# The low halves of the gelu's output: VectorE and GpSimd by turns, or VectorE alone from PSUM

## What is computed

```python
for l in range(attn_w.shape[0]):
    scores = leaky(si[:, :, None] + sj[:, None, :] + attn_b[l])       # masked, softmax
    agg = jnp.einsum('bij,bjd->bid', attn, x)
    h = layernorm(x + agg, g1[l], beta1[l])
    ff = jax.nn.gelu(h @ W1[l] + b1[l], approximate=False) @ W2[l] + b2[l]
    x = layernorm(h + ff, g2[l], beta2[l])
```

## Time and profile before

| | |
|---|---|
| median of 3 runs | 2563.79 us (2563.61 to 2567.0) |
| profiled execution | 2558.94 us |
| its span, first to last instruction | 2557.2 us |
| mean granted TensorE clock | 0.985 of full |
| PE busy | 2299.9 us (90%) |
| DVE busy | 1839.7 us (72%) |
| ACT busy | 1579.6 us (62%) |
| POOL busy | 1274.2 us (50%) |
| chain that ended last | PE 53%, DVE 23%, ACT 8%, issue 8%, POOL 7% |
| low halves on POOL (L657) | 192 of 1182 ns |
| low halves on DVE (L1242) | 192 of 687 ns |

### The profile page before, as it was taken

One profiled execution on the slowest core, in us unless ns is written; L12 is line 12 of the kernel. 1 busy time (PEld: TensorE's weight loads), 2 busy tenths in 40 slices (PEclk: granted clock), 3 DMA queues, 4 the chain that ended last, 5 costly groups with the idle time before them and its releaser, 6 DMA issues.

```text
span 2557.2 us, 41683 instructions
## 1 busy us (share of the span) xinstructions
PE 2299.9 (90%) x14721; PEld 1726.5 (68%) x14721; DVE 1839.7 (72%) x4915; ACT 1579.6 (62%) x2426; POOL 1274.2 (50%) x2199
## 2 busy tenths in 40 slices
PE   5899999997899998999989999899997999999977
PEld 4566666766666766766767767667675677677666
DVE  7676678567677776776877768768677677666775
ACT  5466566655566665665756657565666657666654
POOL 4455455653275453654446533655545456546621
PEclk9999999998999999999999999999999999999998
DMA  6212021101120112100211102111031010001000
GB/s 220 101 42 87 9 87 42 59 1 50 60 89 5 38 50 91 59 18 25 83 59 59 42 3 89 54 54 42 33 109 44 15 42 9 14 29 26 20 23 25
DMA packets 66222, 128.57 MB, mean 50 GB/s; under 512 B 12985, under 2 KB 53213, under 8 KB 62942
## 3 DMA queue, kind: packets, MB, share of 16 engines
q1 hardware_dynamic: 66014, 125.90, 14.8%
HBM read 111.20 MB, written 14.68 MB: 49 GB/s over the span
## 4 chain that ended last, share of the span: by engine, by line
PE 53%; DVE 23%; ACT 8%; issue 8%; POOL 7%; DMA 1%; DVEq 0%; SPq 0%; POOLq 0%; ACTq 0%
PE OB L1595 36%; PE FBB L1595 10%; DVE pw L1228 5%; PE RB L1595 3%; DVE mj L1204 3%; DVE junk L1146 3%; ACT nms L881 2%; DVE st L1095 2%; PE TH L1595 2%; DVE xc L1122 1%; ACT gT L858 1%; POOL rs L626 1%; POOL xc L644 1%; DVE junk L1151 1%; DVE gT L1242 1%
## 5 line engine op out<-in xcount | busy, mean ns | idle before, releaser
L1595 PE MATMUL OB<-xx,pw 128*128 128x257 f32 x4096 | 960.9, 389 | 29.5 <-DVE xc L1122 12.6
L1595 PEld LDWEIGHTS OB<-xx,pw 128*128 128x128 f32 x4096 | 771.5, 193 | 170.0 <-DVE xc L1122 18.9
L1595 PE MATMUL FBB<-hT,wb 128*128 128x512 f16 x2304 | 560.3, 381 | 52.2 <-DVE gT L1242 38.1
L1595 PE MATMUL OB<-wb,gT 128*128 128x256 f16 x4608 | 574.3, 275 | 28.9 <-DVE xc L1122 17.2
L1595 PEld LDWEIGHTS OB<-wb,gT 128*128 128x128 f16 x4608 | 449.6, 99 | 168.1 <-POOL gT L657 22.0
L657 POOL TENSOR_TENSOR gT<-g,gT 128x512 f16<-128x512 f32 x192 | 226.9, 1182 | 538.0 <-ACT gT L858 536.8
L1595 PEld LDWEIGHTS FBB<-hT,wb 128*128 128x128 f16 x2304 | 212.7, 98 | 260.2 <-DVE gT L1242 45.3
L864 ACT ACTIVATE pw<-pw,sj 128x512 f32<-128x512 f32 x512 | 336.4, 712 | 67.5 <-DVE pw L1228 66.7
L1228 DVE SCALAR_TENSOR_TENSOR pw<-r2s,sj,RB 128x512 f32<-128x512 f32 x452 | 319.9, 739 | 43.1 <-PE RB L1595 42.9
L822 ACT ACTIVATE xc<-xc,nb,rs 128x256 f32<-128x256 f32 x384 | 212.6, 590 | 196.0 <-POOL nb L629 196.0
L644 POOL TENSOR_TENSOR xc<-xc,gb 128x256 f32<-128x256 f32 x384 | 293.8, 765 | 16.1 <-ACT xc L822 16.0
(11 more groups left out here) (127 smaller groups left out, 2663.6 us busy)
## 6 DMA issues: line engine op xcount, KB each, us to landing
wb<-w_scratch SPq DMA_DIRECT2D x19, 2048.0 KB, 8.2
adjst<-in_adj SPq DMA_DIRECT2D x56, 512.0 KB, 4.1
xx<-in_x SPq DMA_DIRECT2D x16, 512.0 KB, 5.6
nm<-in_L_gnn_W SPq DMA_DIRECT2D x6, 1024.0 KB, 8.4
gb<-in_L_gnn_g SPq DMA_DIRECT2D x48, 128.0 KB, 2.9
adjst<-in_x SPq DMA_DIRECT2D x6, 1024.0 KB, 11.2
out_x<-adjst SPq DMA_DIRECT2D x48, 128.0 KB, 1.7
pw<-in_adj SPq DMA_DIRECT2D x4, 1024.0 KB, 10.3
```

The costliest lines, as they stand in the source:

```text
L1595: return pe.matmul(o, lhsT, rhs, start=first, stop=last)
```

## The change

VectorE makes the low half of every half-chunk, from PSUM. The odd gelu is written in place in its bank like the even one, GpSimd's `g_low` and the buffer `g32` go, and three waits change: the gelu no longer waits for the previous odd low half; the product into the odd bank waits for the odd low half of two half-chunks before instead of the gelu; and the spread that borrows FBB between steps waits for the odd low halves too.

```diff
-            def g_low(k, n):
-                i = NF * fi(k) + n
-                pool.wait_ge(ghi_done, i + 1)
-                pool.tensor_tensor(out=gT[:, i % GRING, 1, :], in0=g32[:, :], in1=gT[:, i % GRING, 0, :],
-                                   op=ALU.subtract).then_inc(glo_odd, 1)
...
                 src = FB[i % 2][:, :]
-                if n % 2 == 1:
-                    if i >= 2:
-                        act.wait_ge(glo_odd, i // 2)
-                    dst = g32[:, :]
-                else:
-                    dst = src
-                act.activation(dst, src, ACT.Gelu, bias=b1c[:, layer(k), f:f + 1], scale=1.0 / W_SCALE)\
+                act.activation(src, src, ACT.Gelu, bias=b1c[:, layer(k), f:f + 1], scale=1.0 / W_SCALE)\
...
-                act.activation(gT[:, i % GRING, 0, :], dst, ACT.Copy).then_inc(ghi_done, 1)
+                act.activation(gT[:, i % GRING, 0, :], src, ACT.Copy).then_inc(ghi_done, 1)
...
-                                  op=ALU.subtract).then_inc(glo_even, 1)
+                                  op=ALU.subtract).then_inc(glo_odd if n % 2 else glo_even, 1)
...
-                    if n % 2 == 0 and n > 0:
+                    if n > 0:
                         g_low(k, n)
...
                 if i >= 2:
-                    if i % 2 == 0:
-                        pe.wait_ge(glo_even, i // 2)
-                    else:
-                        pe.wait_ge(gelu_done, i - 1)
+                    pe.wait_ge(glo_odd if i % 2 else glo_even, i // 2)
...
-                        pe.wait_ge(gelu_done, NF * fi(q))
+                        pe.wait_ge(glo_odd, NF // 2 * fi(q))
```

More of the change, by code:

```diff
@@ L220, in build @@
         gT = sb("gT", [P, GRING, 2, HALF], f16)
-        g32 = sb("g32", [P, HALF])
         r2s = sb("r2s", [P, N])
@@ L707, in ffn_step @@
                         ln_rstd(LNG, gat, 1)
-                    g_low(k, 1)
                     ln_rstd(LN1, i, 3)
@@ L711, in ffn_step @@
                 for n in range(NF):
-                    if n % 2 == 1 and not (n == 1 and low_first):
-                        g_low(k, n)
                     if n == 11:
```

## The result

The changed kernel took **2547.01 us** in the median of six runs (2543.04 to 2554.98), the kernel before 2563.53 in six (2556.87 to 2567.0). The ratio is 0.9942, 95% interval 0.9925 to 0.9960: the change makes the kernel 10 to 19 us faster. The prediction was 2572, with a range of 2558 to 2584. The same kernel, timed again in a later set (experiment 11), gave 0.9959 (0.9945 to 0.9972).

The account below looks back on a forecast made before the run. TensorE, busy 90%, was taken as the bound, time changing only where it waits. Terms 7 + 3 - 6 + 2 + 0 + 3 = +9, taken as +8.5, gave 2567.4 on the profiled execution, 2572 as median; range 2558 to 2584.

Parts of the forecast that it names:

- steps like 15: Steps 7, 11, 15, 19: GpSimd no longer waits for the n = 3 high half; net -1.6 us each, -6 in sum.
- late passes: Steps 7, 11, 15, 19: passes for n = 9, 11, 13, 15 cost VectorE 2.6 us, some 2 given back.
- steps like 26: Steps 1, 2, 25, 26, 27: product for n = 3 goes 3.0 us late, 1.4 stays; +7 us in sum.
- Step 3: Late n = 1 pass as in step 26, with VectorE dense to the end of the step; +3 us.
- steps like 16: Steps 8, 12, 16, 20, 24, 28: n = 3 product delayed 1.25 us, mostly absorbed; 0.4 lost at n = 11; +2 in sum.
- steps like 17: Steps 9, 13, 17, 21: residuals delayed 0.65 us by the n = 15 pass, some 0.6 won at n = 9; 0.
- Steps 0 and 23: Residual behind the n = 9 pass delays a second product, +0.65 us, and as much at n = 3 or 11; +3.
- all absorbed: Lower bound: no new wait costs TensorE anything and only existing waits go, -17 us.
- Relief wins: Rival, chance 0.15: GpSimd's stops and VectorE collisions go, ten steps like 16 and 17 gain 1 us each; -10 us, 2554.
- Clock: Rival, chance 0.12: 3 us idles in steps like 26 lower TensorE's clock, 1.7 us each, +8.5 on top; 2581.
- It cancels: Rival, chance 0.25: the 1.4 us at n = 1 is eaten by later gaps in the step; +0 to +2, 2564.
- Collisions: VectorE score reductions slowed beside GpSimd low halves; an estimated 29 us of VectorE time comes back.

Follow-up runs that it names:

- experiment 11: The changed kernel unaltered, timed again in a later set: 2552.41 us, ratio 0.9959.
- experiment 7: Kernel before with the change in steps 7, 11, 15 and 19 alone, GpSimd still waiting for each odd high half there: 2557.03 us, ratio 0.9986.
- experiment 6: Kernel before with the low halves for n = 7, 9, 11, 13, 15 of steps 7, 11, 15, 19 given to VectorE: 2563.4 us in one run.
- experiment 2: Changed kernel with the odd low halves of steps 1, 2, 3, 25, 26 and 27 given back to GpSimd: 2543.17 us, ratio 0.9915.
- experiment 8: Changed kernel with 192 extra GpSimd passes at the places of the old ones, waiting for nothing: 2580.97 us, ratio 1.0081.
- experiment 3: Changed kernel with the low half for n = 1 ahead of the row maxima in steps 1, 2, 3, 25, 26, 27: 2541.61 us, ratio 0.9905.
- experiment 10: Changed kernel, odd low halves of steps 1, 2, 3, 25, 26, 27 on GpSimd, residuals ahead of last row maxima in 9, 13, 17, 21: 2541.69 us.
- experiment 4: Kernel before with every odd low half on VectorE but the odd gelu still written to SBUF: 2562.49 us, ratio 0.9991.

## Why the prediction was wrong

- **What failed is the size of the term for the steps like 15.** The mechanism was right (GpSimd's stop at n = 3 held up rstd, nb, ScalarE and a score). The stop itself is worth 1.9 us by experiment 7, where I had 2.0. The error is that I counted only ScalarE's longest wait: another 1.5 us came with it. TensorE's own waits for GpSimd's low half (0.42 and 0.43 us) and the gelu (0.65) went, and the one before n = 4 fell by 0.5; that these are the 1.5 is argued from the trace and not shown by a run. And I charged 0.6 for the late passes, which bring 0.35 (experiment 6). Instead of -1.6 it is -3.3; in step 7, which I had not worked out by itself, -5.2, because a stretch at the lower clock went too. That is 9 of the 19 us by which the sum was off. My own pieces don't even give the -1.6: -2.0, +0.3 and +0.6 are -1.1 a step.
- **The steps like 26** were right in mechanism, place and size: 3.0 us late, 1.3 kept where I had 1.4. Experiment 2 shows that the cost is theirs alone. Their sum is 2 us under the forecast, since step 1 lost its stretch at the lower clock, which it does even where its own passes stay on GpSimd (experiment 2).
- **Step 3** kept 1.1 us in its half-chunks, and the aggregation behind gave it back: 0 for +3. The "densely packed queue" on which I leaned had room.
- **The steps like 16** came out at -0.2 each instead of +0.3. The wait at n = 4 took up only half of the delay of 1.2 us, and the later score kept 1.1 of it up to n = 6; but all of it and 0.5 more had come back by n = 8, which I had put down as "most". The 0.4 of the pass at n = 11 came as said.
- **The steps like 17** were right: 0.1 for 0. They gained 1.5 us in the half-chunks and gave 1.6 back at the residuals, the place that the forecast named.
- **Steps 0 and 23**: 0 for +3, and for step 0 the sign was wrong. I took the wait of 2.47 us of step 23 for both and missed the 4.40 us that TensorE waits for a score in step 0, with the fall of the clock behind it. These went with the change: -2.4 in step 0, and -2.7 in step 1 where the late pass for n = 1 isn't in the way (experiment 2). What in VectorE's queue brings the score sooner was not followed. Step 23 scatters, from -0.5 to +2.4 in the six traces of this kind and from 0 to +1.9 in the five experiments that leave it alone, so no change is shown there.
- **Bounds.** The working had -17 us for "all absorbed", and -10.9 in the profile and 10 to 17 us in the medians lie inside it. The range cut this side off, because the losses that could be seen one by one had weighed more with me than the gains behind them. In the steps like 15 and 16 the losses were costed at their full size and the gains at their largest piece.
- **The rivals.** "Relief wins" had the sign and 0.15. Its place was wrong: the ten steps like 16 and 17, to which it gave 10 us, won 0.2 in sum. Most of the gain sat where the forecast already had one. "Clock" was true as well, and costs 1.7 to 5 us in an execution; but the change also took away stretches at the lower clock, in steps 0, 1 and 7, which no rival had. "It cancels" was not: the 1.3 us at n = 1 stay to the end of the step.
- **Collisions** were under-estimated, 48.6 us given back by the score reductions instead of 29, and by experiment 8 192 more passes on GpSimd without a stop cost the changed kernel some 31 us. The Trainium skill, page "SBUF — State Buffer", section "Who interferes with whom", says that a VectorE instruction with two SBUF inputs contends with a GpSimd instruction that reads SBUF, and that one with at most one, outside the 2-port modes, does not. The traces agree: from PSUM no low half took more than 693 ns, from two inputs in SBUF one took 813 in the mean and up to 1265.

## What to carry to other kernels

Where an engine stands in its queue before an event that comes late, look at what is behind the waiting instruction: here four instructions of 192 held up the statistics of a later stage, and moving these four alone brought as much as the whole change (-15 of -15 us in their steps; the rest of it won 4.0 us in steps 0 and 1 and lost 6.6 in the late ones). When gains and losses are summed, list every wait that a released chain feeds, and not only the longest, with the care given to the losses. A change that wins in one kind of stage and loses in another is best made stage by stage: with the six late stages left out or one pass moved in them the kernel is at 0.9915 and 0.9905 of the time before, instead of 0.994 to 0.996.

## What the hardware showed that I had not expected

- A stop of TensorE of 2.8 us is followed by a stretch at the lower clock in some executions and steps and not in others (one and three of five), at 1.7 us each. This doesn't explain how far apart the runs of a kernel lie: the changed kernel's twelve, with five such stops each, span 12 us, and without the stops experiment 2's four span 3.7, experiment 3's five 7.2 and experiment 10's six 1.0; but the kernel before has no such stops either, and its sets of 13 to 15 runs span 11 to 16.
- In experiment 4 two waits of 2.05 and 2.42 us within 9 us were followed by such a stretch in all four steps of the kind. In the kernel before, the clock fell behind the stop of 4.40 us in step 0 and that of 2.73 us in step 7, and where the change had cut these stops to 1.79 and to 1.06 and 0.99 us it stayed.
- A VectorE edge pass (`nm<-adjst`, one SBUF input, 128x1024) took 0.69 us in the three cases where no GpSimd work overlapped it, and from 0.66 to 1.22 beside GpSimd (over 0.75 in 19 of 56), in the trace of the changed kernel; a low half from PSUM took 0.66 to 0.69 in all 384 cases. The section of the Trainium skill named above ("SBUF — State Buffer", "Who interferes with whom") counts tensor_scalar, which the edge pass is, among the operations that can take the ports that VectorE shares with GpSimd; the trace agrees that it can be slowed beside GpSimd, and doesn't show why in some cases only.
